# Spreading the peak of |g| over the partitions: a transpose of the repeated column in place of an fp32 matmul with the identity

## The reference, cut to what matters

```python
g     = (einsum('bchw,oc->bhwo', x, w_g) + b_g).reshape(B, N, Ci)
theta = (einsum('bchw,oc->bhwo', x, w_theta) + b_theta).reshape(B, N, Ci)
phi   = (einsum('bchw,oc->bohw', x, w_phi) + b_phi[:, None, None]).reshape(B, Ci, N)
att   = softmax(einsum('bnc,bcm->bnm', theta, phi), axis=-1)
y     = einsum('bnm,bmc->bnc', att, g)
out   = einsum('bhwc,oc->bohw', y, w_out) + b_out[:, None, None]
inv   = bn_gamma / sqrt(bn_var + 1e-5)
return x + out * inv + (bn_beta - bn_mean * inv)
```

## Time and profile before

| | us |
|---|---|
| time, median of 3 runs | 224.95 |
| lowest and highest run | 224.67, 225.5 |
| profiled execution, own time | 224.65 |
| profiled execution, span from first to last instruction | 222.8 |

### The profile page before, as it was taken

The page is one execution under the profiler, slowest core; times in us unless marked ns, Lnnn a source line. Parts: engine busy times, 40 slices in busy tenths (PEclk is TensorE's granted clock), DMA queues, the critical chain, the costliest instruction groups (busy, mean ns, idle before and its releaser), DMA issues.

```text
span 222.8 us, 4289 instructions
## 1 busy us (share of the span) xinstructions
PE 214.5 (96%) x1228; PEld 141.5 (63%) x1228; DVE 183.9 (83%) x328; ACT 169.8 (76%) x311; POOL 148.6 (67%) x143
## 2 busy tenths in 40 slices
PE   7997889999999999999999999999999999999994
PEld 6684748656665767657676666647686566656552
DVE  0789998779988699779997799797997799898761
ACT  2687977869688787869698687878878696868751
POOL 2647977786787577966787687866777843843420
PEclk9999999999999999999999999999999999999999
DMA  5107330365106531185104551085200751010102
GB/s 159 72 0 200 79 100 3 108 177 141 47 4 195 135 99 49 43 236 145 47 0 140 151 133 47 0 231 153 61 27 1 188 141 47 0 47 0 50 0 94
DMA packets 8716, 19.78 MB, mean 89 GB/s; under 512 B 1536, under 2 KB 2048, under 8 KB 8704
## 3 DMA queue, kind: packets, MB, share of 16 engines
q1 hardware_dynamic: 8416, 19.50, 31.6%
q10 hardware_dynamic: 288, 0.14, 0.2%
HBM read 4.43 MB, written 4.19 MB: 39 GB/s over the span
## 4 chain that ended last, share of the span: by engine, by line
PE 85%; DVE 6%; DMA 4%; ACT 1%; POOL 1%; issue 0%; SPq 0%; ACTq 0%; DVEq 0%
PE ps_flip L663 25%; PE ps_scores L601 25%; PE ps_y L616 12%; PE ps_y L620 8%; PE ps_misc L628 6%; PE ps_misc L687 4%; PE ps_misc L702 3%; DVE neg_max L496 2%; DMA phi_ll<-lo 2%; DMA vec<-vectors_dram 2%; DVE pt_lo L566 1%; PE ps_misc L607 1%; PE ps_misc L709 1%; DVE phi_ll L484 1%; DVE g_parts L550 1%; ACT L403 1%
## 5 line engine op out<-in xcount | busy, mean ns | idle before, releaser
L316 POOL TENSOR_SCALAR probs<-probs,inv_sum 128x1024 f32<-128x1024 f32 x64 | 72.2, 1127 | 58.3 <-DVE inv_sum L518 58.2
L566 DVE SCALAR_TENSOR_TENSOR pt_lo<-ps_flip,pt_hi 128x512 f16<-128x512 f32 x128 | 82.2, 684 | 25.3 <-ACT pt_hi L446 24.3
L446 ACT ACTIVATE pt_hi<-ps_flip 128x512 f16<-128x512 f32 x128 | 69.7, 597 | 31.6 <-PE ps_flip L663 31.5
L496 DVE TENSOR_REDUCE neg_max<-ps_scores 128x1 f32<-128x1024 f32 x64 | 77.7, 1214 | 0.6 <-PE ps_scores L601 0.5
L663 PEld LDWEIGHTS ps_flip<-ident,probs 128*128 128x128 f32 x512 | 56.9, 141 | 24.7 <-issue 10.3
L455 ACT ACTIVATE probs<-ps_scores,neg_max 128x1024 f32<-128x1024 f32 x64 | 71.8, 1122 | 0.0
L663 PE MATMUL ps_flip<-ident,probs 128*128 128x128 f32 x512 | 68.4, 277 | 3.4 <-POOL probs L316 1.6
L601 PE MATMUL ps_scores<-phi_hh,theta_hl 128*128 128x512 f32 x128 | 45.5, 436 | 0.5 <-DVE phi_ll L484 0.3
L601 PE MATMUL ps_scores<-phi_ll,theta_hl 128*128 128x512 f32 x128 | 40.1, 394 | 0.0
L616 PE MATMUL ps_y<-pt_hi,g_parts 128*128 128x512 f16 (+1 forms) x128 | 32.7, 378 | 0.0
L601 PEld LDWEIGHTS ps_scores<-phi_ll,theta_hl 128*128 128x128 f32 x128 | 24.1, 188 | 5.6
(11 more groups left out here) (77 smaller groups left out, 159.6 us busy)
## 6 DMA issues: line engine op xcount, KB each, us to landing
x_in<-x_in_dram SPq DMA_DIRECT2D x16, 256.0 KB, 3.1
out_dram<-resid SPq DMA_DIRECT2D x15, 256.0 KB, 2.0
phi_hh<-hi SPq DMA_DIRECT2D x14, 256.0 KB, 4.4
phi_ll<-lo SPq DMA_DIRECT2D x14, 256.0 KB, 4.0
theta_hl<-hi SPq DMA_DIRECT2D x7, 256.0 KB, 3.4
theta_hl<-lo SPq DMA_DIRECT2D x7, 256.0 KB, 3.1
out_dram<-resid SPq DMA_DIRECT2D x1, 192.0 KB, 2.0
w_tp<-w_tp_t_dram ACTq DMA_DIRECT2D x1, 128.0 KB, 3.4
```

The lines of the kernel that those rows point to most:

```text
L316: nc.gpsimd.tensor_scalar(out=p[:, :], in0=p[:, :], scalar1=inv_sum[:, at:at + 1], scalar2=1.0, op0=ALU.mult, op1=ALU.mult).then_inc(probs ...
L446: nc.scalar.activation(pt_hi[ring][:, c * HALF_TILES:(c + 1) * HALF_TILES, slot * P:(slot + 1) * P], ps_flip[c][:, :].rearrange("p (a n) - ...
L496: nc.vector.tensor_reduce(out=neg_max[:, k % STEPS:k % STEPS + 1], in_=ps_scores[k % 2][:, :], op=ALU.max, axis=AX.X, negate=True).then_in ...
L566: nc.vector.scalar_tensor_tensor(out=pt_lo[ring][where], in0=ps_flip[c][:, :].rearrange("p (a n) -> p a n", n=P), scalar=PROB_SCALE, in1=p ...
```

## The change

The block is written by a transpose with the repeated column as its data. The repeated column was the stationary operand of the matmul before, and the identity the moving one; in the transposes of this kernel the data (`probs`, `g_channels`) are also stationary and the identity moves. The waits, the semaphore, the target and the place in the order stay as they are.

```diff
             def spread_peak(b, r, target):
                 pe.wait_ge(g_peak_ready, b + 1)
-                nc.tensor.matmul(target, g_peak[:, r:r + 1].to_broadcast([P, P]), ident[:, :],
-                                 start=True, stop=True).then_inc(g_peak_spread, 1)
+                nc.tensor.transpose(target, g_peak[:, r:r + 1].to_broadcast([P, P]),
+                                    ident[:, :]).then_inc(g_peak_spread, 1)
```

## The result

The changed kernel takes 223.84 us (median of 6 runs, 223.76 to 224.11). The kernel before, run beside it, takes 225.06 us (224.63 to 225.5). The ratio is 0.9948 with a 95% interval from 0.9933 to 0.9963, so the kernel is 0.52% faster. A second measurement on another occasion gave 223.64 against 224.73, ratio 0.9948 [0.9933, 0.9963]. The profiled execution took 223.79 us with a span of 221.9.

What follows compares the result with a forecast made beforehand. PE was taken as the bound, unbroken from 59.3 to 188 us. Six boundaries at 0.16, the last at 0.10 and the first call at 0 sum to 1.06 us: 224.95 - 1.06 = 223.9 us, range 223.2 to 224.9.

Steps and rivals of the forecast that it cites:

- The price, 0.16 per call: Spread's cost in PE's chain behind the weighted sum: 0.26 us in place of 0.42, bounds of the gain 0.11 to 0.27.
- record term: One of the fp32 matmul's two records (weight load and matmul) goes from each spread call, worth 0.11 us.
- front term: Exposed load of the first piece behind L620: 0.15 us for a transpose instead of the spread's 0.20, 0.05 less.
- DVE's room, 0.15: At each boundary, DVE's idle time before `pt_lo`, 60.70 to 60.85 us; DVE can move with PE by at most that.
- POOL's slack of 0.51: At the boundary, POOL's scaling ends 0.51 us before PE loads those weights; the gain leaves 0.35 of it.
- The last boundary: Behind 188 us PE's transposes wait for `pt_lo`; an earlier spread gains 0 to 0.14 us, 0.10 taken.
- The first call: Spread call at 15 us, covered by DVE's chain on both sides: gain 0, another 0.11 us were that cover gone.
- Rival 1: At each boundary DVE takes the freed time and PE waits: 224.5 to 224.95 us, 224.7 in the middle; chance 0.14.
- Rival 2: The spread's transposed pass is much cheaper than one fp32 record: 0.20 us gained per call, 223.55 us; chance 0.13.
- Rival 3: The spread's repeated column is slow as transpose data: each call loses 0.09 us, 225.6 us in all; chance 0.05.
- Rival 4: PE's clock falls to 1.2 GHz behind each boundary for the transposes and scores there: 237.6 us; chance 0.01.
- Rival 5: The change does nothing, the spread call leaves two records again: 224.95 us; chance 0.05.

Runs made afterwards that it cites:

- no_spread: The changed kernel without the spread at the seven image boundaries, so the scale of g is off; 223.26 us, ratio 0.9930 to the kernel before.
- two_transposes: The changed kernel with the spread's transpose issued twice into the same block; 224.55 us, ratio 0.9982 to the kernel before.
- early kernels: Spread moved ahead of the weighted sum: in the kernel before 225.36 us, in the changed kernel 224.32 and, repeated, 223.89 us.
- load_transpose: The changed kernel with eight more small DVE instructions at each of the seven boundaries, ahead of `pt_lo`; 224.66 us, ratio 1.0002 to the kernel before.
- first_only: The kernel before with only image 0's spread call made a transpose, the seven boundary calls left fp32 matmuls; 225.03 us, ratio 1.0009.
- after_again: The changed kernel measured once more, unaltered, on another occasion; 223.64 us against 224.73 us for the kernel before, ratio 0.9948.

## Why the prediction was right, point by point

- **The count of records** (8 for 16): as predicted.
- **PE is the bound at the boundaries up to 162 us:** right. The windows are full, and no_spread shows that even 0.10 more was kept there.
- **The price, 0.16 per call:** 0.17 measured (0.42 to 0.25, 25.67 to 25.50). Its record term, 0.11, was shown by two_transposes (0.11 to 0.12) and by the first boundary of the early kernels (0.22 against 0.11). Its front term, 0.05, is the shorter load (187 to 133 ns): the next record starts 0.053 earlier. The term was taken from a transpose of `probs` behind L620, whose load is 139 ns; the one of the repeated column is shorter, which no row of before showed.
- **DVE's room, 0.15:** too small. It was read from the end of L544's record, but DVE starts the next instruction before that: 0.05 us behind L544's start in no_spread, and 0.06 between the small instructions of load_transpose (8 in 0.48). The room was about 0.24, so all of the 0.17 fitted in. Behind it stood the slack between `pt_lo` and the transposes that wait for it, which the prediction didn't count; load_transpose found where it ends.
- **POOL's slack of 0.51:** no wait appeared, as predicted.
- **The last boundary, 0.10 taken between 0 and 0.14:** mis-sized. It kept 0.17. The bound of 0.14 was read in the same way, from the end of L544's record (189.04) to the start of `pt_lo` (189.18). By 0.05 behind L544's start it would have been 0.23. `pt_lo` still followed the start of `pt_hi` by 0.63 us there, before and after, so it moved with PE by the whole.
- **The first call, 0:** right, by first_only and the unchanged 21.8 us from tile 0's scores to tile 8's.
- **The sum:** 7 x 0.17 = 1.19 measured from the traces, 1.06 predicted, 1.17 by the ratio (0.0052 x 225.06) and 1.22 by the medians. The small excess is the last boundary and 0.01 on each of the others. The bound of 1.21 held the traces' sum, but only because the 0.11 it allowed for the first call covered what the other terms lacked. That the median came within 0.1 us of the 223.9 foreseen is partly luck: the kernel before, measured beside it, was 0.11 slower than the 224.95 from which the gain was taken, and its gain by the medians 0.16 larger than forecast; the two nearly cancel. On the other hand I gave "within 0.5%" more than "faster by over 0.5%"; the ratio of 0.9948 lies just on the faster side, with the line inside its interval.
- **Rival 1** (absorbed by DVE) is false for this kernel and mostly true for one with 0.48 us more work on DVE at the boundary. **Rival 2** (a much cheaper pass) is false: the transposed record keeps a cost of 0.11 and streams like one fp32 record, and the "4×" of the Trainium skill ("TensorE: Matmul & The Clock Gate", Terms) doesn't show at 128 columns, where two records became one. **Rival 3** is false, a step of zero costs the transpose's load nothing (133 ns against 141). **Rival 4**: the mean clock of the profiled execution after is 0.999, and 1.00 in both windows up to 188 us. Only behind 188 us does it read 0.98; after_again has 1.000 throughout with the same time. So it is no effect of the change that shows in the time. (The 30% of transposes in the chain doesn't stand in the earlier trace rows; from one L709 to the next the pieces of L663 and L709 add up to 7.9 of 25.67 us.) **Rival 5** is false.

## What to carry to other kernels

Price a small PE operation by the distance to the next piece in the chain, and split it into records and the load that its neighbours can't hide; a plain fp32 matmul that only copies or spreads values leaves two records, a transpose or a matmul in fp32r or 16 bits one. Before counting a gain on a full engine, follow who is just behind it: here 0.17 us came through whole, and with half a us more on DVE only 0.03 of it did at most boundaries. Don't read an engine's room from the end of a record when its records overlap; look for how closely two instructions follow each other elsewhere (0.05 us here, where the record was 0.13 long). An operation moved to hide its load can meet a wait that was over in its old place.

## What the runs showed of the hardware that was not expected

- The weight load of the transposed, repeated column takes 133 ns; a block of `probs` takes 141, the same column in a plain fp32 matmul 187, in fp32r 185, in bf16 96.
- An fp32 pair of 64 moving columns isn't 0.11 us cheaper than one of 128, nor equal, but 0.06 cheaper: the first record is 0.053 cheaper, the second not at all.
- The first record behind L620 starts 0.31 us behind L620's last, whether it is an fp32, transposed, fp32r or bf16 one (0.309 to 0.312). What its load and its columns move is the start of the next record. So a bf16 matmul put there costs next to nothing (0.02 us in the chain): it takes the gap on itself, and the transposes behind it add 0.88 instead of the 1.02 that they add directly behind L620. What makes the gap no run here shows.
